# First block of an x-times-weight product reordered by kind of product, with a zero product ahead of it, in a shared-plus-routed expert kernel

## The chip, the cores and the metric

The kernel runs on one core of one Trainium2 chip. The metric is the device time of one execution in microseconds (us); of several runs the median is given. One further execution was recorded by the hardware profiler, and all rows below are from that one.

The engines are named as in the profile: PE is TensorE (matmul), PEld its weight load, DVE is VectorE, ACT is ScalarE, POOL is GpSimd, SP is SyncE, which here only issues DMAs. A q behind a name (SPq) is the engine's instruction queue issuing a DMA.

## The reference

The input x is 4 x 1024 tokens of 512 numbers. Two layers are added to it:

```
ys  = cond / sqrt(512)                                # [4, 512]
d   = rsqrt((ys*ys) @ (W*W) + 1e-8)                   # demodulation, [4, 512]
x1  = x + ((x * ys) @ W) * d                          # W is 512 x 512
shared = (silu(x1 @ w1) * (x1 @ w3)) @ w2             # 512 -> 1024 -> 512
s      = sigmoid([x1, cond] @ router_W)               # 8 experts
top 2 of s + bias per token, gates = s normalised over the two
routed = sum over the two experts of gate * (gelu(x1 @ W1e) @ W2e)
out = x1 + (shared + routed) / 3
```

All of it is fp32.

## The kernel before

Every large fp32 product is made of three products of fp32r operands: each operand is split into a high part (ACT copies it with rounding) and a low part (DVE subtracts the high part from the original), and PE adds high\*high, high\*low and low\*high in one bank of PSUM. So every tile of x, of a weight or of a hidden state passes ACT and then DVE before PE may use it.

**Stage 1, the first linear layer**: 8 blocks (NBLK) of 512 tokens. For a block, PE makes 4 output chunks o of 128 features, each from 4 input chunks c, three products each: 48 matmuls of 128x512. The first block is written apart in `first_linear` (loop over c outside, since its inputs arrive chunk by chunk), the others in `linear` (loop over o outside). Both call `part`, lines 416 to 418. After chunk c = 2 of the first block PE runs `demodulation` (line 399): 16 small fp32 products of the squared weight w0sq, made by POOL (line 1138), with the squared scales modsq. They show as 32 rows in the trace, with 4 columns each. ACT makes the weight's high parts wmh (line 583) and the block's high parts xh (`x_high`, line 575), and DVE the low parts wml (line 735) and xl (`scaled_low`, line 730). Before anything else both need mod, the scaled condition, which DVE makes (line 718) out of the load of cnd that SP issues first (line 235). ACT's queue waits for `prep` before its first high part.

The results leave PSUM by DVE at line 762 (x1t, one instruction for each o) into SBUF, PE then makes the router logits of the block (line 448), and SP stores x1t to HBM and loads the block after next into xin. In the last two blocks of the stage SP loads instead blocks 0 and 1 of the stored x1t back into xin, for stage 2; so in the last block (n = 7) ACT and DVE make the high and low parts of stage 2's first block (`x_low`, line 725). The tuple at line 764 says after which o DVE makes which low parts: none after o = 0 and 1, c = 0 after o = 2, and c = 1, 2, 3 after o = 3.

**Stage 2, the shared layer**: for each of 8 blocks, 8 hidden chunks hc. PE runs `up` (lines 468 to 470, 24 matmuls), then `down` of the hidden chunk before (lines 482 to 484, 12 matmuls). Between the two a hidden chunk passes ACT (silu, line 611), DVE (gate, line 792), ACT (high part gh, line 616) and DVE (low part gl, line 796). The order on each engine is fixed by the program; nothing is reordered at run time.

Beside it, ACT and DVE split the experts' weights for stage 3 in 32 pieces. In blocks 0 and 1 one piece goes with each hidden chunk: `piece_high` on ACT (line 631), `piece_low` on DVE (line 994), each at the end of the step of its hidden chunk. SP's `move_piece` loads a piece (line 302) and stores the split one (line 304). SP loads piece 0 at line 269, once the first two quarters of w2 are split. The load of a later piece needs that the piece two before it has been stored, since both use one buffer. In hidden chunk 1 of block 0 ACT also makes the router's sigmoid, for which it must load another table, and then the first one again for the silu after it. In block 1 DVE also works out the routing tables (lines 856 to 987).

**Stage 3, the routed experts**: 71 tiles of 128 gathered tokens, lines 530 to 532 on PE, with POOL gathering and scatter-adding rows.

Of the kernel before, what the change touches and what calls it, by code (L numbers as in the profile page):

```python
# [13 lines left out]
P = 128  # L14
# [51 lines left out]
def shared_moe_kernel(nc, xT, w0, condT, router_w, router_b, shared_w, expert_w, consts, tokid, padslots, padrows, out):  # L66
# [8 lines left out]
    with ctx:  # L75
        base = -(-nc.sbuf_base // 128) * 128

        def sb(name, shape, dt, kib):
            return nc.alloc_sbuf_tensor_at(name, [P] + shape, dt, offset=base + int(kib * KIB))
# [3 lines left out]


        x1t = sb("x1t", [2, DC, BLK], FP32, 0)
        w13 = sb("w13", [HC, 2, 2 * DC * P], FP32R, 16)
        wmh = sb("wmh", [2, DC, D], FP32R, 80)
        wml = sb("wml", [2, DC, D], FP32R, 96)
# [91 lines left out]
        cond_in = sem("cond_in")  # L180
        w0_in = [sem(f"w0_in{c}") for c in range(DC)]
        x0_in = [sem(f"x0_in{c}") for c in range(DC)]
        square_done = sem("square_done")
        pads_in = sem("pads_in")
        xin_in = [sem(f"xin_in{j}") for j in range(2)]
        wraw_in = [sem(f"wraw_in{j}") for j in range(2)]
# [44 lines left out]
        def _(sp):  # L231
            for j in range(2):
                sp.sem_inc(x1t_out[j], 16)
                sp.sem_inc(ehl_out[j], 16)
            sp.dma_start(cnd[:, :, :], condT).then_inc(cond_in, 16)
            for c in range(DC):
                sp.dma_start(w0s[:, c, :], w0[:, c, :]).then_inc(w0_in[c], 16)
            sp.sem_inc(xin_in[0], 16)
# [150 lines left out]
        def _(pe):  # L389
# [30 lines left out]
            def first_linear():  # L420

                for c in range(DC):
                    pe.wait_ge(wml_ready, c + 1)
                    pe.wait_ge(xl_ready, c + 1)
                    for o in range(DC):
                        last = part(0, o, c, 0)
                        if c == DC - 1:
                            last.then_inc(lin_done, 1)
                    if c == DC - 2:
                        demodulation()  # L430
# [12 lines left out]
            def logits(n, j):  # L443
# [5 lines left out]
                                         x1t[:, j, o, s * P:(s + 1) * P], start=(o == 0), stop=(o == DC - 1))  # L449
                last.then_inc(log_done, 1)  # L450

            first_linear()
            for n in range(1, NBLK):
                linear(n, n % 2)
# [117 lines left out]
        def _(act):  # L572
# [69 lines left out]
            for hc in range(HC):  # L642
                gate(0, hc)
                if hc == 1:
                    act.wait_ge(logit_done, 1)
                    act.activation(score[:, :, :], score[:, :, :], ACT.Sigmoid).then_inc(score_done, 1)
                next_high(0, hc, 0, NBLK // 2)
                hidden_high(0, hc)
                if hc in (0, 2, 4):
                    w2_high(1 + hc // 2)  # L650
                piece_high(0, hc)
            block_steps(1, 1, NBLK // 2 + 1)

            with act.Fori(1, NBLK // 2 - 1) as h:
# [48 lines left out]
        def _(dve):  # L703
# [10 lines left out]
            dve.sem_inc(xgt_done, 2)  # L714
            dve.sem_inc(hidt_done, 2)
            dve.sem_inc(ys_done, 2)
            dve.wait_ge(cond_in, 16)
            dve.tensor_scalar(mod[:, :, :], cnd[:, :, :], float(np.float32(1.0) / np.sqrt(np.float32(D))), None, ALU.mult).then_inc(prep, 1)
            dve.wait_ge(prep, 1)
# [13 lines left out]
            for c in range(DC):  # L733
                dve.wait_ge(wmh_ready, c + 1)
                dve.tensor_tensor(wml[:, 0, c, :], w0s[:, c, :], wmh[:, 0, c, :].bitcast(FP32), ALU.subtract).then_inc(wml_ready, 1)
                scaled_low(0, c)
            for c in range(DC):
                scaled_low(1, c)
            dve.wait_ge(small_in, 64)
# [13 lines left out]
            for n in range(NBLK):  # L753
                j = n % 2
                for o in range(DC):

                    dve.wait_ge(lin_done, DC * n + o + 1 + 1)
                    if o == 0:
                        dve.wait_ge(x1t_out[j], 16 * (n // 2) + 16)
                        if n > 1:  # L760
                            dve.wait_ge(log_done, n - 1)
                    dve.scalar_tensor_tensor(x1t[:, j, o, :], lin_ps[(DC * n + o) % 5][:, :], dsc[:, o, n // 2:n // 2 + 1],
                                             xin[:, j, o, :], ALU.mult, ALU.add).then_inc(x1t_done, 1)
                    for c in (() if n == 0 else ((), (), (0,), (1, 2, 3))[o]):
                        if n + 1 < NBLK:
                            scaled_low(n + 1, c)
                        else:
                            x_low(n + 1, (n + 1) % 2, c)
                dve.wait_ge(w_high, n + 1)
                dve.tensor_tensor(w13[:, n, 1, :], wraw[:, j, :], w13[:, n, 0, :].bitcast(FP32), ALU.subtract).then_inc(w_split, 1)  # L770
# [225 lines left out]
            for hc in range(HC):  # L996
                block_step(0, hc, 0, True)
                if hc < 2:
                    turn_x1(0, 0, 2 * hc)
                    turn_x1(0, 0, 2 * hc + 1)  # L1000
                if hc in (0, 2, 4):
                    w2_low(1 + hc // 2)
                if hc == 5:
                    dve.wait_ge(score_done, 1)
                    then(dve.tensor_tensor(row(SEL), score[:, :, :], per_expert(rb[:, :]), ALU.add))
                if hc == 6:
                    choose(0)
                if hc == 7:
                    choose(1)
                piece_low(0, hc)  # L1010
            for hc in range(HC):
                block_step(1, hc, 1, True)
                if hc == 0:
# [96 lines left out]
        def _(pool):  # L1110
# [22 lines left out]

                pool.wait_ge(xrow_out[i % XB], 16 * K * (i // XB + 1))

            for c in range(DC):
                pool.wait_ge(w0_in[c], 16)
                pool.tensor_tensor(w0sq[:, c, :], w0s[:, c, :], w0s[:, c, :], ALU.mult).then_inc(square_done, 1)
            pool.wait_ge(tables_done, 3)
            pool.wait_ge(sadr_done, K)  # L1140
            pool.wait_ge(pad_done, 1)
# [110 lines left out]
```

## Time and profile before

| | us |
|---|---|
| median of 3 runs | 1060.47 (1059.27 to 1061.65) |
| the profiled execution, its own time | 1054.4 |
| span of its trace (first to last instruction) | 1052.6 |
| PE busy in the span | 1021.2 |
| stage 1 on PE | 10.4 to 113.9 |
| stage 2 on PE | 115.8 to about 645 |
| stage 3 and the end | to 1052.6 |

The trace rows give a start and a duration in us from the start of the span. A matmul row's duration overlaps the next one's, so the pace of matmuls is read from the distance of their starts: 0.43 us at TensorE's clock of 1.2 GHz and 0.227 us at 2.4 GHz for 128x512. The profiled execution was 6.1 us shorter than the median of the runs; differences are made against its own rows and then taken off the median.

### The profile page before, as it was taken

What the parts mean: (1) busy time and instruction counts of PE and PEld (TensorE: products, weight loads), DVE (VectorE), ACT (ScalarE), POOL (GpSimd) and SP (SyncE); (2) the same over time, 40 slices, a digit from 0 to 9 for tenths busy, and PEclk for the clock granted to TensorE, in tenths of its full rate; (3) what the DMA queues carried; (4) which work ended last, traced back from release to release, by engine and by line L of the source; (5) the groups of instructions that cost most, each with busy time, mean ns of one, the idle gap of its engine ahead of it and who ended that gap; (6) DMA issues with size and microseconds to landing.
All of it is one profiled execution on the core that took longest, in us unless ns stands there. A gap on an engine that the chain in (4) does not pass through costs nothing.

```text
span 1052.6 us, 14602 instructions
## 1 busy us (share of the span) xinstructions
PE 1021.2 (97%) x4692; PEld 836.1 (79%) x4692; DVE 506.2 (48%) x828; ACT 293.0 (28%) x461; POOL 331.5 (31%) x393
## 2 busy tenths in 40 slices
PE   6999999999999999999999998999999999999996
PEld 5888778887888888888888886788888888878874
DVE  4555456668333333333322214555655566555653
ACT  3222252332222222122211112333333233332331
POOL 2000000001214433334312401365554645545533
PEclk9999999999999999999999999999999999999999
DMA  4666688787876677876833576999778999999984
GB/s 172 200 206 217 222 281 255 259 318 248 294 239 233 221 267 253 264 268 212 290 100 90 190 202 205 239 221 231 147 147 179 226 221 231 210 215 226 228 180 80
DMA packets 133259, 228.61 MB, mean 217 GB/s; under 512 B 29041, under 2 KB 83953, under 8 KB 125105
## 3 DMA queue, kind: packets, MB, share of 16 engines
q1 hardware_dynamic: 60400, 144.06, 42.8%
q0 software_dynamic: 31328, 64.11, 26.4%
q10 hardware_dynamic: 41472, 19.68, 7.9%
q8 instruction: 35, 0.57, 0.2%
q14 instruction: 24, 0.19, 0.1%
HBM read 112.85 MB, written 98.38 MB: 201 GB/s over the span
## 4 chain that ended last, share of the span: by engine, by line
PE 83%; DMA 8%; DVE 4%; SPq 2%; issue 2%; ACT 1%; POOLq 0%; DVEq 0%
PE banks L530 13%; PE banks L532 12%; PE banks L531 12%; PE banks L468 8%; PE banks L469 8%; PE banks L470 8%; DMA we_d<-ehl 5%; PE banks L482 4%; PE banks L483 4%; PE banks L484 4%; PE banks L416 3%; PE banks L417 3%; PE banks L418 3%; DMA eraw<-expert_w 2%; SPq L286 1%
## 5 line engine op out<-in xcount | busy, mean ns | idle before, releaser
L468 PE MATMUL banks<-xh,w 128*128 128x512 f32 x512 | 199.6, 390 | 1.8 <-DVE xl L725 1.8
L469 PE MATMUL banks<-xl,w 128*128 128x512 f32 x512 | 199.2, 389 | 0.0
L470 PE MATMUL banks<-xh,w 128*128 128x512 f32 x512 | 199.2, 389 | 0.0
L1184 POOL DMA_INDIRECT out<-ys,slot x71 | 124.0, 1746 | 181.1 <-DVE ys L1080 89.4
L792 DVE SCALAR_TENSOR_TENSOR gm<-sil,banks 128x512 f32<-128x512 f32 x64 | 43.9, 685 | 240.7 <-ACT sil L611 234.6
L1073 DVE TENSOR_TENSOR hidtl<-hidt,hidth 128x512 fp32r<-128x512 f32 x71 | 49.1, 692 | 165.9 <-ACT hidth L685 165.2
L611 ACT ACTIVATE sil<-banks 128x512 f32<-128x512 f32 x64 | 38.2, 597 | 291.9 <-PE banks L470 291.9
L1170 POOL DMA_DIRECT2D xg<-xs_d x136 | 99.9, 1108 | 58.8 <-DVE xgt L1054 49.6
L530 PE MATMUL banks<-we,hidth 128*128 x284 | 112.2, 395 | 5.8 <-issue 5.5
L530 PE MATMUL banks<-we,xgth 128*128 x284 | 111.1, 391 | 3.4 <-issue 3.4
L468 PEld LDWEIGHTS banks<-xh,w 128*128 128x128 f32 x512 | 96.1, 188 | 22.3 <-issue 2.3
L470 PEld LDWEIGHTS banks<-xh,w 128*128 128x128 f32 x512 | 96.1, 188 | 19.9
L469 PEld LDWEIGHTS banks<-xl,w 128*128 128x128 f32 x512 | 96.1, 188 | 19.8
L532 PE MATMUL banks<-we,hidtl 128*128 x284 | 110.7, 390 | 0.0
L531 PE MATMUL banks<-we,hidth 128*128 x284 | 110.7, 390 | 0.0
L531 PE MATMUL banks<-we,xgth 128*128 x284 | 110.5, 389 | 0.0
L532 PE MATMUL banks<-we,xgtl 128*128 x284 | 110.5, 389 | 0.0
L482 PE MATMUL banks<-wmh,gh 128*128 128x512 f32 x256 | 99.9, 390 | 2.8 <-DVE gl L796 1.7
L685 ACT ACTIVATE hidth<-hidt 128x512 fp32r<-128x512 f32 x71 | 44.9, 632 | 200.8 <-PE banks L532 131.1
L483 PE MATMUL banks<-wml,gh 128*128 128x512 f32 x256 | 99.6, 389 | 0.0
L484 PE MATMUL banks<-wmh,gl 128*128 128x512 f32 x256 | 99.6, 389 | 0.0
L1142 POOL DMA_DIRECT2D xrow<-padrows x1 | 0.8, 766 | 244.7 <-DVE place_of L987 244.7
(163 smaller groups left out, 1512.0 us busy)
## 6 DMA issues: line engine op xcount, KB each, us to landing
we_d<-ehl SPq DMA_DIRECT2D x32, 1024.0 KB, 7.3
we<-we_d SPq DMA_DIRECT2D x48, 512.0 KB
hturn<-hid ACTq DMA_DIRECT2D x284, 64.0 KB
xg<-xs_d POOLq DMA_DIRECT2D x136, 128.0 KB
eraw<-expert_w SPq DMA_DIRECT2D x32, 512.0 KB
x1t_d<-x1t SPq DMA_DIRECT2D x8, 1024.0 KB, 8.8
xin<-x1t_d SPq DMA_DIRECT2D x8, 1024.0 KB, 8.8
x_d<-x1tok SPq DMA_DIRECT2D x32, 256.0 KB
```

Of the source, the lines that this page charges most:

```text
L468: pe.matmul(ps[hc % 2][:, :], w_hi, xh[:, j, c, :], start=(c == 0), stop=False)
L469: pe.matmul(ps[hc % 2][:, :], w_hi, xl[:, j, c, :], start=False, stop=False)
L470: last = pe.matmul(ps[hc % 2][:, :], w_lo, xh[:, j, c, :], start=False, stop=(c == DC - 1))
L482: pe.matmul(o_ps[s][:, :], g_hi, w2h[:, hc, :], start=(hc == 0), stop=False)
L483: pe.matmul(o_ps[s][:, :], g_hi, w2l[:, hc, :], start=False, stop=False)
L484: last = pe.matmul(o_ps[s][:, :], g_lo, w2h[:, hc, :], start=False, stop=(hc == HC - 1))
L530: pe.matmul(ps, high[:, c, :], w_hi, start=(c == 0), stop=False)
L531: pe.matmul(ps, high[:, c, :], w_lo, start=False, stop=False)
L532: last = pe.matmul(ps, low[:, c, :], w_hi, start=False, stop=(c == DC - 1))
L1073: dve.tensor_tensor(hidtl[:, t % 2], hidt[:, t % 2], hidth[:, t % 2].bitcast(FP32), ALU.subtract).then_inc(hidt_done, 1)
L1170: pool.dma_start(xg[g * Q:(g + 1) * Q, m % 2 * PAIR:(m % 2 + 1) * PAIR].rearrange("p t a n -> p (t a) n"), xs_d[m * PAIR * P:(m + 1) * PAI ...
L1184: pool.indirect_dma_start(out[:, :], IO(slot[:, t, 0:1], 0), ys[:, t % RING, :], None, compute_op=ALU.add).then_inc(added[t % 2], 16)
```

## The change

1. **First block by kind of product.** `first_linear` issues for each c first the four products wmh\*xh (they wait for wmh and xh only), then the four wml\*xh (after a wait for wml), then the four wmh\*xl (after a wait for xl).
2. **Zeros.** DVE's first instruction fills a new tile of 128x512 with zeros (it shares its place with x1t), and PE starts with 20 matmuls of 128x512 on it, into the bank of lin_ps[4].
3. **Squares.** The four squares w0sq move from POOL to DVE, behind the low parts of the first block and ahead of those of the second.
4. **Condition.** The load of cnd is issued by POOL, no longer by SP ahead of the weight's loads.
5. **Low parts in the last block.** In block 7 of stage 1 DVE makes the low part c = o right after x1t of o, for each o.
6. **First piece.** Piece 0 of the experts' weights is split at the end of hidden chunk 1, right ahead of piece 1, and no longer at the end of hidden chunk 0, on ACT and on DVE.

```diff
+        zeros = sb("zeros", [BLK], FP32R, 0)
@@ sync
-            sp.dma_start(cnd[:, :, :], condT).then_inc(cond_in, 16)
@@ tensor
                 for c in range(DC):
+                    pe.wait_ge(wmh_ready, c + 1)
+                    pe.wait_ge(xh_ready, c + 1)
+                    for o in range(DC):
+                        pe.matmul(lin_ps[o][:, :], wmh[:, 0, c, o * P:(o + 1) * P], xh[:, 0, c, :], start=(c == 0), stop=False)
                     pe.wait_ge(wml_ready, c + 1)
+                    for o in range(DC):
+                        pe.matmul(lin_ps[o][:, :], wml[:, 0, c, o * P:(o + 1) * P], xh[:, 0, c, :], start=False, stop=False)
                     pe.wait_ge(xl_ready, c + 1)
                     for o in range(DC):
-                        last = part(0, o, c, 0)
+                        last = pe.matmul(lin_ps[o][:, :], wmh[:, 0, c, o * P:(o + 1) * P], xl[:, 0, c, :], start=False, stop=(c == DC - 1))
...
+            pe.wait_ge(zeros_done, 1)
+            for _ in range(20):
+                pe.matmul(lin_ps[4][:, :], zeros[:, 0:P], zeros[:, :], start=True, stop=True)
             first_linear()
@@ scalar
-                piece_high(0, hc)
+                if hc == 1:
+                    piece_high(0, 0)
+                if hc:
+                    piece_high(0, hc)
@@ vector
+            dve.memset(zeros[:, :].bitcast(FP32), 0.0).then_inc(zeros_done, 1)
             dve.wait_ge(cond_in, 16)
...
+            for c in range(DC):
+                dve.tensor_tensor(w0sq[:, c, :], w0s[:, c, :], w0s[:, c, :], ALU.mult).then_inc(square_done, 1)
...
-                    for c in (() if n == 0 else ((), (), (0,), (1, 2, 3))[o]):
+                    for c in (() if n == 0 else (o,) if n == NBLK - 1 else ((), (), (0,), (1, 2, 3))[o]):
...
-                piece_low(0, hc)
+                if hc == 1:
+                    piece_low(0, 0)
+                if hc:
+                    piece_low(0, hc)
@@ gpsimd
-            for c in range(DC):
-                pool.wait_ge(w0_in[c], 16)
-                pool.tensor_tensor(w0sq[:, c, :], w0s[:, c, :], w0s[:, c, :], ALU.mult).then_inc(square_done, 1)
+            pool.dma_start(cnd[:, :, :], condT).then_inc(cond_in, 16)
```

The order of instructions on PE at its start, before (the first 7 rows; "banks" are PSUM banks):

```order
L388 UNCONDITIONAL_BRANCH
L416 MATMUL banks<-xh,wmh 128x512
L417 MATMUL banks<-xl,wmh 128x512
L418 MATMUL banks<-xh,wml 128x512
L416 MATMUL banks<-xh,wmh 128x512
L417 MATMUL banks<-xl,wmh 128x512
L418 MATMUL banks<-xh,wml 128x512
```

and now:

```order
L388 UNCONDITIONAL_BRANCH
L460 MATMUL banks<-zeros 128x512 x20
L426 MATMUL banks<-xh,wmh 128x512 x4
L429 MATMUL banks<-xh,wml 128x512 x4
L432 MATMUL banks<-xl,wmh 128x512 x4
L426 MATMUL banks<-xh,wmh 128x512 x4
L429 MATMUL banks<-xh,wml 128x512 x4
L432 MATMUL banks<-xl,wmh 128x512 x4
```

The first product with xl stood second and now stands ninth among the products of the block, behind 20 of zeros.

The order on ACT from the first hidden chunk's high part on, before (ehl is the split piece, wmh here the high part of a quarter of w2):

```order
L631 ACTIVATE ehl<-eraw 128x1024
L611 ACTIVATE sil<-banks 128x512
L646 ACT_TABLE_LOAD
L646 ACTIVATE score<-score 128x256
L616 ACTIVATE gh<-gm 128x512
L631 ACTIVATE ehl<-eraw 128x1024
L611 ACT_TABLE_LOAD
```

and now:

```order
L620 ACTIVATE sil<-banks 128x512
L655 ACT_TABLE_LOAD
L655 ACTIVATE score<-score 128x256
L625 ACTIVATE gh<-gm 128x512
L640 ACTIVATE ehl<-eraw 128x1024 x2
L620 ACT_TABLE_LOAD
```

The piece that stood ahead of the silu of hidden chunk 1 now stands behind its high part gh.

## Rows read from the trace of the kernel before

**Rows 1.** PE's waits, whole span: us in total, times, longest.
```profile
PE banks L416 <- DVE xl L730: 10.4, 1, 10.4
...
PE banks L468 <- DVE xl L725: 1.8, 1, 1.8
PE banks L482 <- DVE gl L796: 1.7, 1, 1.7
PE banks L482 <- DVE outst L804: 1.0, 1, 1.0
```
**Rows 2.** Timeline from the start: start, duration, engine, line, what.
```profile
1.02 0.39 SPq L235 DMA_DIRECT2D cnd<-condT  x1
...
4.17 0.18 DVE L718 TENSOR_SCALAR mod<-cnd 128x16 f32<-128x16 f32 x1 [4.17 <-DMA cnd<-condT]
...
7.20 0.63 ACT L583 ACTIVATE wmh<-w0s 128x512 fp32r<-128x512 f32 x1 [2.40 <-DMA w0s<-w]
7.25 5.38 POOL L1138 TENSOR_TENSOR w0sq<-w0s 128x512 f32<-128x512 f32 x4 [6.79 <-DMA w0s<-w]
7.74 0.71 ACT L575 ACTIVATE xh<-xin,mod 128x512 fp32r<-128x512 f32 x1
...
8.76 1.52 DVE L730 SCALAR_TENSOR_TENSOR xl<-xin,mod,xh 128x512 fp32r<-128x512 f32 x1
...
10.43 0.77 PE L416 MATMUL banks<-xh,wmh 128*128 128x512 f32 x1 [10.43 <-DVE xl L730]
...
11.28 0.71 ACT L575 ACTIVATE xh<-xin,mod 128x512 fp32r<-128x512 f32 x1
...
14.37 0.68 DVE L735 TENSOR_TENSOR wml<-w0s,wmh 128x512 fp32r<-128x512 f32 x1
```
**Rows 3.** The same timeline: PE after its start.
```profile
14.27 0.39 PE L416 MATMUL banks<-xh,wmh 128*128 128x512 f32 x1
...
20.41 3.63 PE L399 MATMUL banks<-modsq,w0sq 128*128 128x4 f32 x32
```
**Rows 4.** Stretch: length, busy PE, PEld, DVE, ACT, POOL, then clock, DMA share, GB/s.
```profile
24.00:27.70 3.70, 3.70 (x11) 2.87 (x11) 2.63 (x8) 1.16 (x2) 0.00 (x0) 0.54 0.02 4
```
**Rows 5.** Chain of waits, end of block 0, start of block 2: start, duration.
```profile
28.27 0.23 PE banks L418
...
41.22 0.43 PE banks L416
```
**Rows 6.** ACT's timeline, third block's high parts.
```profile
36.20 2.56 ACT L575 ACTIVATE xh<-xin,mod 128x512 fp32r<-128x512 f32 x4 [10.75 <-DMA xin<-xT]
```
**Rows 7.** Timeline of the end of stage 1, ACT and DVE.
```profile
108.23 2.19 ACT L575 ACTIVATE xh<-xin 128x512 fp32r<-128x512 f32 x4 [8.36 <-DMA xin<-x1t_d]
...
112.94 0.75 DVE L762 SCALAR_TENSOR_TENSOR x1t<-banks,dsc,xin 128x512 f32<-128x512 f32 x1 [1.37 <-PE banks L418]
...
113.61 1.88 DVE L725 TENSOR_TENSOR xl<-xin,xh 128x512 fp32r<-128x512 f32 x3
...
115.75 0.47 PE L468 MATMUL banks<-xh,w 128*128 128x512 f32 x1 [1.84 <-DVE xl L725]
```
**Rows 8.** ACT's timeline in hidden chunks 0 and 1 of block 0.
```profile
133.36 1.06 ACT L631 ACTIVATE ehl<-eraw 128x1024 fp32r<-128x1024 f32 x1 [6.62 <-DMA eraw<-expert_w]
```
**Rows 9.** PE's timeline, the same place.
```profile
138.03 0.47 PE L482 MATMUL banks<-wmh,gh 128*128 128x512 f32 x1 [1.74 <-DVE gl L796]
```
**Rows 10.** SP's DMA issues, pieces 2 (load) and 1 (store).
```profile
139.59 0.33 SPq L302 DMA_DIRECT2D eraw<-expert_w  x1
140.23 0.35 SPq L304 DMA_DIRECT2D we_d<-ehl  x1
```
**Rows 11.** Chain of waits, 112 to 270 us: shares by line.
```profile
by line: DMA we_d<-ehl 34.5%; DMA eraw<-expert_w 10.1%; SPq L286 7.0%; DVE ehl L994 4.5%; issue 3.3%; SPq L302 2.9%; ACT gh L616 2.4%; PE banks L468 2.3%; DVE gl L796 2.2%; PE banks L469 2.2%; ACT ehl L631 2.0%; PE banks L470 2.0%; DVE gm L
```
**Rows 12.** Stretch of the input loads, columns as in Rows 4.
```profile
12.00:14.00 2.00, 2.00 (x7) 1.52 (x6) 2.00 (x3) 0.27 (x1) 0.63 (x1) 1.00 0.99 401
```
**Rows 13.** DMA issues by kind: KB each, median us from issue to landing.
```profile
xrow<-padslots POOLq DMA_DIRECT2D x1, 1.0 KB, 6.9
```

More of the change, by code:

```diff
@@ L182, in shared_moe_kernel @@
         x0_in = [sem(f"x0_in{c}") for c in range(DC)]
-        square_done = sem("square_done")
+        square_done, zeros_done = sem("square_done"), sem("zeros_done")
         pads_in = sem("pads_in")
```

## The prediction

> **What bounds the kernel now.** I read PE's waits over the whole span first [rows 1]. PE waits for another engine four times in 1052.6 us: 10.4 us for its first input, 1.8 at the end of stage 1, 1.7 in the first hidden chunks of stage 2 and 1.0 at 262 us. So PE bounds nearly everything; whatever makes it reach the later stages sooner shortens the run, unless something that doesn't move with PE then holds it back. The change touches the first three waits, and the fourth matters for what part of the gain stays.
>
> Next I read the timeline from the start [rows 2]. The first product needs no low part, but the program waits for one: xh of chunk 0 is ready at 7.74 + 0.71 = 8.45 us, xl at 8.76 + 1.52 = 10.28, and PE starts at 10.43. Then the pace [rows 3]: PE's tenth matmul starts at 14.27, so nine took 3.84 us, 0.427 each, which is TensorE at its lower clock of 1.2 GHz after an idle stretch. The other 27 up to the small products at 20.41 took 6.14 us, 0.227 each, which is 2.4 GHz. After 3.63 us of small products the clock is down again: the granted clock of 24.0 to 27.7 is 0.54 [rows 4], and the last chunk's twelve matmuls need from 20.41 + 3.63 = 24.04 to 28.27 + 0.23 = 28.50 [rows 3, 5], 4.46 us where 12 x 0.227 = 2.73 would do.
>
> **Part by part.**
>
> *By kind of product, with the condition's load moved.* PE may start 0.15 us after xh (the distance from xl to the first product now): 8.45 + 0.15 = 8.60, 1.83 us earlier. At full clock a chunk takes 12 x 0.227 = 2.73 us. Inputs come faster: the last xh ends at 11.28 + 0.71 = 11.99 [rows 2], while PE wants it at 8.60 + 3 x 2.73 plus the small products, after 20 us. The low parts of chunk 0 are wanted 0.9 and 1.8 us after the start, at 9.5 and 10.4; even with xl as slow as now, 10.28, it is in time. SP's queue is 0.4 us freer without cnd (issued at 1.02 now, [rows 2]), but the DMA engines are full while the inputs land (share 0.99, [rows 12]), so I take nothing for it; bounds 0 and 0.4. Chunk 0's weight load lands shortly ahead of 7.20, and cnd at 4.17, so cnd has slack: mod, its square (0.18 each) and one small ACT instruction of about 0.2 have to be done by 7.20, so it may land up to 6.5.
>
> *Zeros.* DVE's memset can run about when SP issues its first DMA, 1.02 us. The trace has no memset of this size; its nearest row, a DVE operation of 128x512 with two inputs, is 0.68 [rows 2], and a tiny one 0.18. So the zeros on PE start at about 1.5. If TensorE's clock rises as it did, 3.84 us after the start, nine take 3.84 us and eleven 2.50: they end at 7.8, ahead of 8.60. If it never rose they would take 20 x 0.427 = 8.54 and end at 10.0. I take the first: then the nine slow matmuls of the block are gone, 3.84 - 9 x 0.227 = 1.80 us. The gap up to 8.60 is 0.8 us; PE idled for 1.84 and 1.74 us further on, and the first matmul behind them took 0.47 [rows 7, 9], not the 0.77 of the cold start [rows 2]; so such a gap keeps the clock.
>
> *Squares on DVE.* Four times 0.68 behind the last xl. That one ends about 0.1 + 0.74 after the last xh, at 12.9 (DVE is no longer slowed to 1.52 beside POOL; 0.74 for one is my estimate from 0.68), so the squares are done at 15.6, and PE comes to them at 8.60 + 36 x 0.227 = 16.8. Cost nothing; without that 1.2 us of cover each microsecond would be one of PE's. The low parts of block 1 come 2.7 us later, at about 18.6; PE wants them after the last chunk, at about 24.9.
>
> *The clock after the small products.* They stay where they are, 3.63 us of 4-column matmuls, so I leave the dip in: gain 0, with 4.46 - 2.73 = 1.73 as the other bound. First block in all: 1.83 + 1.80 = **3.6 us**. The results now come out together at the end of the last chunk, so x1t of o = 3 is some 2 us later against PE than now, and with it the reload of xin, on which ACT's high parts of block 2 wait (they start at 36.20 and take 2.56, [rows 6]). Their shift is 1.5 us instead of 3.6. PE starts block 2 at 41.22 [rows 5] and needs the second low part three matmuls on, at 41.9 - 3.6 = 38.3. The second high part ends at 36.20 - 1.5 + 1.28 = 36.0, and behind it DVE has x1t of o = 3 and then this low part, 0.75 and 0.74 at most: 37.5. Cost nothing, with little to spare: 0.8 us.
>
> *Last block of stage 1.* Now three low parts stand behind the last x1t: 113.61 + 1.88 = 115.49, PE 115.75 [rows 7]. With one (a third, 0.63 to 0.68) they end at 114.3 and PE starts at 114.55: **1.2 us**. The cost is a wait: DVE, after x1t of o = 0, stands until ACT's first high part at about 108.23 + 0.6 = 108.8, with x1t of o = 1 to 3 queued behind. Six operations of 0.6 to 0.7 (low, x1t, low, x1t, low, and room) follow by 112.2, and x1t of o = 3 isn't due before 112.94. Cover 0.7 us; beyond it, the reload being late costs one for one.
>
> *First piece.* ACT's piece 0 waits for its load until 133.36 [rows 8], ahead of the silu of hidden chunk 1, and for the low part gl of that chunk PE waits 1.74 us, until 138.03 [rows 9]. Moved behind, silu to gl need no DMA and the wait goes: 1.7 us. But what follows in blocks 0 and 1 is not PE's pace: in the chain from 112 to 270 us the DMAs of pieces hold 34.5 + 10.1% [rows 11], and it ends in DVE's routing tables and outst at 262, for which PE already waits 1.0 us. This chain starts at piece 0's load, which shifts with stage 1's gains but not with this one. Its first links: piece 1 is stored at 140.23, and could be at best shortly after 139.59, when piece 0's buffer is free [rows 10]. So the chain gains some 0.3, PE comes 1.7 earlier, and the wait of 1.0 grows to about 2.4. I take **0.3 us**, bounds 0 and 1.7.
>
> **Sum**: 1.83 + 1.80 + 1.2 + 0.3 = 5.1 us. The profiled execution's 1054.4 becomes 1049.3. The median of the runs was 1060.47; I take the same difference off it: **1055.4**.
>
> **A page against the trace.** The dip after the small products is what the row shows [rows 4]. The Trainium skill (TensorE: Matmul & The Clock Gate, Part 1) says the gate's observation runs freely and isn't tied to the kernel's start. By that rule, with the small products now 3.6 us earlier, the dip can fall otherwise or not at all; no row here shows it.
>
> **The rivals.**
>
> *A. The clock stays up through the small products.* They begin 16.8 us in, with work on both sides. Then 1.73 us more: 6.8 in all, 1053.7. Against it: the same products in the same length did bring it down. Chance 0.17.
>
> *B. Zeros don't raise the clock.* They end at 10.0, the block starts there, 0.4 us earlier than now, and its nine slow matmuls remain: 0.4 + 1.2 + 0.3 = 1.9 us, 1058.6. For it: no row shows a product of zeros. Against: PE's array has the same work to do. Chance 0.09.
>
> *C. The gain is taken back later.* A chain beside PE (pieces in blocks 0 and 1, weights in stage 3) doesn't shift with stage 1. Then PE's wait at 262 grows by the whole gain, to about 6 us, and the time is 1060 to 1060.5. Against: piece 0's load waits for w2's parts, which follow PE. Chance 0.08.
>
> *D. Slower: the condition on POOL's queue.* Everything on ACT stands behind mod. If cnd lands later than 6.5, each microsecond is one of start. The nearest row of that queue is 6.9 from issue to landing [rows 13]: landing at about 8, a loss of 1.5, still a gain of 3.6 in all. It turns if its packets must wait until the input loads are through (still 0.99 busy at 12 to 14, [rows 12]). Landing at 15: the start comes 8.5 us later than forecast, and the clock has fallen in the idle stretch, 1.8 more. 5.1 - 10.3 = -5.2: 1065.7. It decides from a landing at 11.6 on. Chance 0.04. The Trainium skill (DMA: Bandwidth & Descriptors, Latency and other measured facts) puts the first byte of a POOL-issued DMA at 1 us against 0.6, so by the page it would be only 0.4 later, within the slack.
>
> **How the numbers follow.** Forecast 0.62, A 0.17, B 0.09, C 0.08, D 0.04. About 2.1 us (0.2%) is what a measurement of this kernel can tell from no change. Forecast and A are faster, of B half (it stands at the bound), C is the same: faster 0.84, same 0.12, slower 0.04. The range: at the lower end A with the piece's 1.7 kept, 1060.5 - 8.2 = 1052.3, less 1.3 for the spread of the runs; at the upper end B with 1.2 of spread. Range 1051.0 to 1059.8; D and part of C lie outside.
>
> **What would show it.** In the profile after: zeros from about 1.5 to 7.8 with the step from 0.43 to 0.227 between; the first real product at 8.6 and 0.227 apart; small products at about 16.8, again a clock near 0.54 behind them; end of the first block at 24.9; PE's wait ahead of up at 0.6 or less; no wait at line 482 for gl near 134, and one of about 2.4 us for outst near 258. Wrong would be: cnd landing after 6.5, zeros at 0.43 throughout, a PE wait for x1t or xl in block 2, or a wait for outst of 1.0 (then the piece's gain is whole).

## The result and the profile after

| | before | changed |
|---|---|---|
| median of 8 runs, us | 1061.18 (1058.67 to 1065.06) | 1055.68 (1052.02 to 1060.37) |
| ratio | | 0.9945, 95% interval 0.992 to 0.997 |
| profiled execution, span | 1052.6 | 1058.6 |

The changed kernel is faster by 5.5 us, by the interval 3.2 to 8.5. The forecast of 1055.4 lies 0.3 us off the median; that it is so near is partly luck, as the terms show below. But the one profiled execution of the changed kernel is 6 us longer than that of before, so the sum can't be read off two spans; it has to be followed from stage to stage.

PE's waits over the whole span (us in total, times, longest), which answer to [rows 1]:

```profile
PE banks L539 <- issue: 12.0, 22, 2.3
PE banks L491 <- DVE outst L819: 3.0, 2, 2.1
PE banks L460 <- DVE zeros L729: 1.9, 1, 1.9
PE banks L539 <- SPq L340: 1.5, 1, 1.5
PE banks L477 <- DVE xl L738: 0.6, 1, 0.6
PE banks L426 <- ACT xh L584: 0.6, 1, 0.6
```

The wait for gl is gone, the one for xl is 0.6 instead of 1.8, and the one for outst has grown from one of 1.0 to two of 3.0 together. The start, from the timeline (start, duration, engine, line, what), against [rows 2]:

```profile
1.32 0.75 POOL L1154 DMA_DIRECT2D cnd<-condT  x1 [0.85 <-POOLq L1262]
1.40 0.48 DVE L729 MEMSET zeros<- 128x512 f32 x1 [1.40 <-PEq L1262]
1.94 6.98 PE L460 MATMUL banks<-zeros 128*128 128x512 f32 x20 [1.94 <-DVE zeros L729]
...
7.57 0.17 DVE L731 TENSOR_SCALAR mod<-cnd 128x16 f32<-128x16 f32 x1 [5.69 <-DMA cnd<-condT]
...
8.63 0.70 ACT L584 ACTIVATE xh<-xin,mod 128x512 fp32r<-128x512 f32 x1
...
9.48 1.16 PE L426 MATMUL banks<-xh,wmh 128*128 128x512 f32 x4 [0.56 <-ACT xh L584]
...
17.75 4.56 PE L399 MATMUL banks<-modsq,w0sq 128*128 128x4 f32 x32
```

The condition lands 6.2 us after POOL issues it, at 7.5 instead of 4.1, and ACT's first high part, which no longer waits for the weight, waits for it: the block starts at 9.48, not at 8.60. Then it runs at full pace at once (four products in 1.16). After the small products comes the dip, in stretches as in [rows 4] (length, busy PE, PEld, DVE, ACT, POOL, then granted clock, DMA share, GB/s):

```profile
17.80:20.00 2.20, 2.20 (x22) 2.20 (x21) 1.38 (x3) 0.00 (x0) 0.00 (x0) 1.00 0.00 0
20.00:22.20 2.20, 2.20 (x14) 2.20 (x13) 0.00 (x0) 0.00 (x0) 0.00 (x0) 0.55 0.03 7
...
25.70:27.20 1.50, 1.50 (x5) 1.18 (x4) 0.74 (x2) 0.00 (x0) 0.00 (x0) 0.55 0.00 0
```

It begins already among the small products, which take 4.56 us instead of 3.63, and takes in all twelve products of the last chunk: the clock is at half from 20.2 to 27.1 us, against 24.3 to 27.7 in the kernel before.

**Milestones on PE**, us from the span's start (first row of each kind), for the two kernels and for the two repetitions described below:

| | before | before again (f1) | changed | changed again (e1) |
|---|---|---|---|---|
| first real product | 10.43 | 10.54 | 9.48 | 9.25 |
| logits of the condition (after block 1) | 39.24 | 39.29 | 38.17 | 36.37 |
| first product of stage 2 | 115.75 | 115.80 | 113.48 | 111.68 |
| first product of stage 3 | 643.89 | 643.99 | 641.91 | 640.09 |
| from there to the end of the span | 408.7 | 411.5 | 416.7 | 412.1 |

Stages 1 and 2 repeat to 0.1 us in the kernel before, and differ by 1.8 us in the changed one. Stage 3 scatters by 8 us; in the longest of these four the chain of waits runs through its DMAs and scatter-adds:

```profile
1019.96 4.30 DMA out<-ys,slot
...
1030.68 5.42 DMA out<-ys,slot
```

So all runs below are read by these milestones first, and by their times second.

### The profile page after: what moved, and what is told of

The parts are those of the page before. It is cut to its first block, busy times and chain, and to the rows that moved or that the text cites. A ratio compares the mean times of both kernels' runs of the same rounds, so it can differ in the third digit from the quotient of the medians.

```text
span 1058.6 us, 14641 instructions
## 1 busy us (share of the span) xinstructions
PE 1031.7 (97%) x4712; PEld 842.4 (80%) x4712; DVE 505.7 (48%) x833; ACT 292.0 (28%) x461; POOL 332.0 (31%) x390
## 4 chain that ended last, share of the span: by engine, by line
PE 69%; DMA 17%; issue 4%; DVE 4%; SPq 2%; POOL 1%; ACT 1%; ACTq 1%; POOLq 0%; DVEq 0%
PE banks L539 11%; PE banks L540 10%; PE banks L541 10%; PE banks L477 6%; PE banks L479 6%; PE banks L478 6%; DMA we_d<-ehl 6%; DMA we<-we_d 4%; PE banks L491 3%; PE banks L493 3%; PE banks L492 3%; PE banks L416 3%; PE banks L417 2%; PE banks L418 2%; DMA xs_d<-xrow,sadr 2%
```

## The experiments

Twelve experiments ran, two of them repetitions, each with 5 rounds of timed runs (9 or 12 runs of each). Ratios are against the kernel before on the same chip. "After" in the diffs is the changed kernel.

**e1, the changed kernel again.**

> The changed kernel once more, to see what repeats. Theory M (stages 1 and 2 carry the gain, stage 3 only scatters): first real product within 0.3 us of 9.5, up to the first product of stage 2 at 113.5 +- 2 depending on where the clock falls, first product of stage 3 at 642 +- 2, and the length of stage 3 anywhere in 407 to 417 us; time 1053 to 1058. Rival S (the change also shortens stage 3): stage 3 here is 404 to 406 us.

1053.75 us against 1058.31, ratio 0.9951 (0.9933 to 0.997). Milestones as above: theory M holds, stage 3 isn't shortened (412.1). The dip here starts only behind the small products and ends inside the next block:

```profile
19.00:21.00 2.00, 2.00 (x20) 2.00 (x20) 0.97 (x3) 0.00 (x0) 0.00 (x0) 1.00 0.03 8
21.00:23.00 2.00, 2.00 (x9) 1.67 (x9) 1.13 (x6) 1.17 (x2) 0.00 (x0) 0.81 0.00 0
23.00:25.00 2.00, 2.00 (x6) 1.54 (x6) 0.70 (x2) 0.00 (x0) 0.00 (x0) 0.50 0.00 0
25.00:26.00 1.00, 1.00 (x5) 0.78 (x4) 1.00 (x3) 0.00 (x0) 0.00 (x0) 0.67 0.00 0
```

Same program, same work, 1.8 us between the two. Of that, 0.2 us is the start; the other 1.6 is the dip, which lasted from 22.3 to 25.7 us here and from 20.2 to 27.1 in the first trace. So it is mainly how long the clock stayed down, and not only where it fell.

**e2, the condition's load on SP.**

```diff
+            sp.dma_start(cnd[:, :, :], condT).then_inc(cond_in, 16)
             for c in range(DC):
                 sp.dma_start(w0s[:, c, :], w0[:, c, :]).then_inc(w0_in[c], 16)
...
-            pool.dma_start(cnd[:, :, :], condT).then_inc(cond_in, 16)
```

> The changed kernel with the condition's load issued by SP again, ahead of the weight's loads. Theory Q (POOL's queue delivers the condition late, at 7.5 us, and that costs the start): the first real product at 8.6 +- 0.2, 0.9 us earlier than in the changed kernel, and the first product of stage 2 earlier by about as much if the clock falls at the same place. Rival W (the start is set by the weight's first load, which SP now issues 0.4 us later): first real product still at 9.2 to 9.5.

Its timeline from the start:

```profile
1.95 6.47 PE L461 MATMUL banks<-zeros 128*128 128x512 f32 x20 [1.95 <-DVE zeros L730]
...
4.06 0.18 DVE L732 TENSOR_SCALAR mod<-cnd 128x16 f32<-128x16 f32 x1 [2.17 <-DMA cnd<-condT]
...
6.97 0.63 ACT L593 ACTIVATE wmh<-w0s 128x512 fp32r<-128x512 f32 x1 [2.27 <-DMA w0s<-w]
...
7.50 0.71 ACT L585 ACTIVATE xh<-xin,mod 128x512 fp32r<-128x512 f32 x1
```

Theory Q holds: the condition is there at 4.1, ACT waits for the weight again, xh ends at 8.21, and PE starts at 8.36, 1.1 and 0.9 us ahead of the two traces of the changed kernel. Moving this one small load cost the start about 1 us. But e2 puts back two things at once: the queue, and the place ahead of the weight's loads. Other small loads in the changed kernel's trace, issued by SP behind the weight's, were as slow (DMA issues by kind: KB each, median us from issue to landing):

```profile
rw<-router_w SPq DMA_DIRECT2D x1, 32.0 KB, 7.5
cnd<-condT POOLq DMA_DIRECT2D x1, 8.0 KB, 6.2
rb<-router_b SPq DMA_DIRECT2D x1, 4.0 KB, 6.3
```

In the kernel before, SP's rb took 5.9 us too, while cnd, which SP issued first of all, took 3.1. So the place behind the large loads may explain all of it. The load on SP behind the weight's, which would tell the two apart, wasn't run. The time, 1055.02 (ratio 0.9957, 0.9938 to 0.9976), doesn't show it: this trace had the long dip (logits of the condition at 37.02), and a microsecond is less than the interval.

**e3, no zeros.**

```diff
-            pe.wait_ge(zeros_done, 1)
-            for _ in range(20):
-                pe.matmul(lin_ps[4][:, :], zeros[:, 0:P], zeros[:, :], start=True, stop=True)
```

> The changed kernel without its 20 products of zeros. Theory Z (the zeros raise the clock): the block's first 8 to 10 products 0.427 us apart, the small products start 1.8 us later than in the changed kernel, at 19.6, and stage 2 starts up to 1.8 us later, less if the dip behind the small products becomes shorter. Rival (the first products would be at the higher clock anyway): small products at 17.8.

PE's timeline at its start:

```profile
9.32 2.04 PE L426 MATMUL banks<-xh,wmh 128*128 128x512 f32 x4 [9.32 <-ACT xh L581]
11.16 1.72 PE L429 MATMUL banks<-xh,wml 128*128 128x512 f32 x4
```

Theory Z holds: the first four products take 1.84 us from start to start instead of about 1.0, and the small products come at 19.08, against 17.54 in e1 and 17.75. From the first real product to the first small one it is 9.76 us, against 8.29 and 8.27: 1.5 us. So products of zeros raise the clock as products of data do. What is left at stage 3 is less clear: it starts at 640.76, between the two traces of the changed kernel, since the dip behind was a short one and the waits for outst were 2.1 us instead of 3.0. Time 1054.63, ratio 0.9974 (0.9954 to 0.9993); the intervals of e1 and e3 overlap.

**e4, the small products dealt out.**

```diff
                     for o in range(DC):
                         pe.matmul(lin_ps[o][:, :], wmh[:, 0, c, o * P:(o + 1) * P], xh[:, 0, c, :], start=(c == 0), stop=False)
+                        if c == DC - 1:
+                            next(small, None)
...
+                        if c == DC - 1:
+                            next(small, None)
+                            next(small, None)
...
-                    if c == DC - 2:
-                        demodulation()
+                        if c == DC - 2:
+                            next(small, None)
```

(`small` is the list of the 16 products, taken one by one; the first four stand behind the last four matmuls of chunk 2.)

> The changed kernel with the 16 small products of the demodulation dealt out among the last four matmuls of chunk 2 and the first eight of chunk 3, one or two behind each. Theory D (a stretch of nothing but 4-column products lets the clock fall): no granted clock under 0.9 between 15 and 30 us, and the first block ends at 24.6 or sooner, against 27.3 in the changed kernel. Rival (the small products are as light wherever they stand, so the mixed stretch lets the clock fall too): clock near 0.5 again for some 3 us, end of the first block 26.5 or later.

The stretches behind chunk 2, columns as above:

```profile
17.00:19.00 2.00, 2.00 (x16) 1.80 (x14) 2.00 (x4) 0.91 (x2) 0.00 (x0) 1.00 0.01 4
19.00:21.00 2.00, 2.00 (x17) 1.84 (x15) 0.30 (x2) 0.00 (x0) 0.00 (x0) 1.00 0.04 8
21.00:23.00 2.00, 2.00 (x17) 1.86 (x17) 0.00 (x0) 0.00 (x0) 0.00 (x0) 1.00 0.00 0
23.00:25.00 2.00, 2.00 (x11) 1.70 (x11) 1.23 (x7) 1.17 (x2) 0.00 (x0) 1.00 0.00 0
```

No dip; the first block ends at 24.15 (theory D asked for 24.6 or sooner), logits of the condition at 35.04, stage 3 at 637.17. Time 1053.6, ratio 0.9951 (0.9933 to 0.997), the same as e1's on the same chip: the timed runs don't show this gain. By itself one trace proves little, as f4 below shows; g1 to g4 repeat it.

**f1, the kernel before again.**

> The kernel before once more, unchanged. Theory L (the one trace of before that the forecast used was a fast one in stages 1 and 2, since the clock's dip varied): the first product of stage 3 comes later than that trace's 643.9 us, by up to 1.5 us. Rival: 643.9 +- 0.3, and what the timed runs show beyond 2 to 4 us lies in stage 3.

Theory L falls: 643.99, as in the first trace. Time 1060.32 against 1058.82 on that chip, ratio 1.0016 (0.9996 to 1.0036): this much two sets of runs of one kernel differ.

**f2, the first piece in its old place.**

```diff
-                if hc == 1:
-                    piece_high(0, 0)
-                if hc:
-                    piece_high(0, hc)
+                piece_high(0, hc)
```

and the same for `piece_low`.

> The changed kernel with the first piece split at the end of hidden chunk 0 again. Theory G (what the moved piece gains is given back at the wait for outst near 258): the wait for gl of 1.7 us near 134 is back, the waits for outst near 190 and 258 shrink together from 2.9 to about 1.2, and from the first product of stage 2 to the first of stage 3 it takes 528.4 +- 0.4 us as in the changed kernel. Rival K (the gain is kept): the waits for outst stay near 2.9 and that stretch takes 530.1.

PE's timeline where it waits in stage 2:

```profile
134.13 0.47 PE L491 MATMUL banks<-wmh,gh 128*128 128x512 f32 x1 [1.86 <-DVE gl L808]
...
258.40 0.50 PE L491 MATMUL banks<-wmh,gh 128*128 128x512 f32 x1 [0.73 <-DVE outst L816]
```

Theory G holds: the wait for gl is back (1.86), the one near 190 is gone and the one near 258 is 0.73 (1.2 was expected). From the first product of stage 2 to the first of stage 3 it takes 528.00 us, against 528.43 and 528.41 in the changed kernel, and 528.14 and 528.19 in the kernel before. What the moved piece gains at 134 is given back in full. The 0.4 us between f2 and the changed kernel says nothing more: with the piece moved and stage 2 otherwise the same program, this stretch was 526.8 to 528.5 us over seven traces (changed, e1 to e4, g3, g4), 528.0 in the mean; with the piece in its old place it was 528.0 to 528.2 in three. Time 1057.27, ratio 0.9982 (0.9954 to 1.0009), which is the slowest of the variants. Its trace doesn't say why (stage 3 was 407.9). Its timed runs also had the lowest granted clock of all variants, 0.993 in the median against 0.995 in e1, but whether that explains it is open.

**f3, the old low parts in the last block.**

```diff
-                    for c in (() if n == 0 else (o,) if n == NBLK - 1 else ((), (), (0,), (1, 2, 3))[o]):
+                    for c in (() if n == 0 else ((), (), (0,), (1, 2, 3))[o]):
```

> The changed kernel with the low parts of the last block of stage 1 in their old places. Forecast's theory: PE waits 1.8 us for xl ahead of stage 2, against 0.6, so from the first logits of the condition to the first product of stage 2 it takes 76.5 us, against 75.3. The 1.2 us are kept to stage 3, because the chain of pieces starts behind it. Rival: the early low parts only move a wait, and the stretch stays at 75.3 to 75.6.

The stretch from the logits of the condition to stage 2 takes 76.51 us, as in both traces of before, against 75.3 in the changed kernel and all its other variants: 1.20 us, as forecast. Part of it may not last: the waits for outst were 0.6 us less here, in one trace. And stage 2 held a surprise. It took 529.67 us, and not for waits (2.4 us for outst, against 3.0 in the changed kernel). PE's timeline at the start of stage 2, and the stretches from there, columns as above:

```profile
114.89 0.47 PE L477 MATMUL banks<-xh,w 128*128 128x512 f32 x1 [1.84 <-DVE xl L738]
```

```profile
115.00:116.00 1.00, 1.00 (x5) 0.82 (x6) 1.00 (x2) 0.00 (x0) 0.00 (x0) 1.00 0.96 311
116.00:117.00 1.00, 1.00 (x5) 0.76 (x4) 1.00 (x2) 0.00 (x0) 0.00 (x0) 0.60 1.15 295
117.00:118.00 1.00, 1.00 (x4) 0.81 (x3) 0.01 (x1) 0.00 (x0) 0.00 (x0) 0.50 0.83 188
```

About a microsecond behind the idle stretch of 1.84 us (ahead of which PE ran a microsecond of router logits) the clock fell to half, until about 119.6. That cost about 1.8 us: 529.67 - 528.43 + 0.56. The two traces of before have the same gap without this dip [rows 7], and none of the eleven traces with a gap of 0.6 us there has it. One case in three is a hint that the longer gap is to blame; it doesn't show it. Time 1056.43, ratio 0.9976 (0.9958 to 0.9994).

**f4, the tables earlier.**

```diff
-                if hc == 5:
+                if hc == 3:
                     pe.wait_ge(mask_done, 1)
-                    pe.wait_ge(gm_done, HC + 4 + 1 + 2)
+                    pe.wait_ge(gm_done, HC + 2 + 1 + 2)
...
-                if hc == 5:
-                    first_slots()
-                if hc == 6:
-                    slot_rows()
-                    pad_rows()
-                if hc == 7:
-                    turns()
-                    tile_tables()
+                if hc == 3:
+                    first_slots()
...
+                if hc == 7:
+                    tile_tables()
```

(slot_rows, pad_rows and turns at hc 4, 5 and 6; the rank is taken over at hc 2.)

> The changed kernel with the routing tables of block 1 made two hidden chunks earlier and spread over five (rank at chunk 3, then one part of the tables at each chunk). Theory V (the wait for outst near 258 is set by VectorE's table work behind a late piece): that wait falls from 2.0 to under 0.3 us and stage 3 starts 1.5 to 2 us earlier. Rival P (the pieces' DMAs alone set it): it stays at 1.5 or more.

The wait near 258 stays at 1.64 us: rival P. Behind it stands the piece on both engines, in ScalarE's and VectorE's timelines:

```profile
250.43 1.06 ACT L640 ACTIVATE ehl<-eraw 128x1024 fp32r<-128x1024 f32 x1 [8.35 <-DMA eraw<-expert_w]
```

```profile
251.53 1.22 DVE L1009 TENSOR_TENSOR ehl<-eraw,ehl 128x1024 fp32r<-128x1024 f32 x1 [5.83 <-ACT ehl L640]
...
254.66 2.48 DVE L819 TENSOR_TENSOR outst<-banks,xres 128x512 f32<-128x512 f32 x4
```

VectorE was free 5.83 us ahead of it, waiting for ScalarE, and that 8.35 us for the load. And this trace has no dip after the small products, which stand together as in the changed kernel (they took 3.63 us, logits of the condition at 34.92). Time 1054.06, ratio 0.9958 (0.9933 to 0.9982).

**g1 to g4** all have the small products dealt out as in e4.

**g1** adds f4's tables and moves the last pieces of blocks 0 and 1 behind the output:

```diff
                 if hc == 0:
                     output(0)
+                    piece_low(0, HC - 1)
...
+                            if 2 * h + j == 2:
+                                piece_low(1, HC - 1)
```

with ScalarE's `piece_high` in the matching place.

> The changed kernel with the small products dealt out as in e4, the tables made earlier as in f4, and the last pieces of blocks 0 and 1 split behind the outputs of the block before, in hidden chunk 0 of the next block, no longer ahead of them (the loops over blocks 2 to 5 on ScalarE and VectorE are written out for that). Theory H (a late piece, standing ahead of the output on both engines, sets both waits for outst): both waits are under 0.3 us, and from the first product of stage 2 to the first of stage 3 it takes 525.5 +- 0.6 us, against 528.4; stage 3 starts at 635.5 to 636.5. Rival R (the residual's load or the pieces' DMAs hold the output themselves): waits for outst of 1 us or more remain. For the clock: by theory D no dip between 15 and 30 us, a second case beside e4.

From PE's waits over the span:

```profile
PE banks L499 <- DVE gl L821: 0.7, 1, 0.7
```

No wait for outst is left, only this one for gl; stage 2 takes 525.80 us, 2.6 less than in the changed kernel and 1.0 less than the shortest of the seven traces named at f2. Theory H holds: a late piece ahead of the output made both waits. The tables alone don't remove them (f4 kept 1.23 us near 189 and 1.64 near 257); whether the moved pieces would without the tables wasn't run. 1052.41 us, ratio 0.9943 (0.9916 to 0.997).

**g2** is g1 with e2's edit.

> g1 with the condition's load on SP. By theories Q, D and H together: first real product at 8.4 to 8.6, no dip, first product of stage 3 at 634.5 to 635.5, 7 us ahead of the changed kernel's first trace, and a time 3 to 6 us under the changed kernel's. Rival (what is gained by stage 3 is lost in it, since its length follows its DMAs): stage 3 takes 412 us or more and the time is that of the changed kernel, 1053 to 1056.

No wait for gl or outst at all, stage 2 in 524.88 us, stage 3 from 634.84: 7.1 us ahead of the changed kernel's first trace and 9.1 ahead of before. 1050.76 us, ratio 0.9923 (0.9895 to 0.995): the lowest of all, 8 us under the kernel before. Stage 3 took 414.1 us in its trace, so the rival's first half came true, but the time stayed under its 1053 to 1056: g3, which ran on the same chip with the late pieces and the tables in their old places, took 1053.28. The start fell short, see g3.

**g3** is the changed kernel with e4's and e2's edits alone.

> The changed kernel with the small products dealt out and the condition's load on SP, nothing else. Theories Q and D: first real product at 8.4 to 8.6, no dip between 15 and 30 us, logits of the condition at 34.0 +- 0.3, against 38.2 and 36.4 in the two traces of the changed kernel. Rival to D (it was chance that e4 had no dip, as f4 had none with the small products together): a granted clock near 0.5 somewhere between 15 and 30 us here or in g1, g2 or g4.

Its timeline from the start:

```profile
1.94 7.33 PE L469 MATMUL banks<-zeros 128*128 128x512 f32 x20 [1.94 <-DVE zeros L738]
...
8.06 0.71 ACT L593 ACTIVATE xh<-xin,mod 128x512 fp32r<-128x512 f32 x1
...
9.11 1.08 PE L430 MATMUL banks<-xh,wmh 128*128 128x512 f32 x4
```

No dip, logits of the condition at 34.53, 0.5 us later than expected. PE started at 9.11 though xh was ready at 8.77, since the 20 zeros ran until then (a row's duration overlaps the next one's); in g2 they held the start to 9.24 with xh ready at 8.11. How long 20 zeros take depends on when the clock rises: 6.33 us in e1, 7.46 in g2. With the condition on SP they can be too many: in e2, where they took 6.47, they cost nothing. 1053.28 us, ratio 0.9945 (0.9923 to 0.9967).

**g4** is the changed kernel with e4's edit and the squares on POOL, behind the condition's load:

```diff
             pool.dma_start(cnd[:, :, :], condT).then_inc(cond_in, 16)
+            for c in range(DC):
+                pool.wait_ge(w0_in[c], 16)
+                pool.tensor_tensor(w0sq[:, c, :], w0s[:, c, :], w0s[:, c, :], ALU.mult).then_inc(square_done, 1)
```

> The changed kernel with the small products dealt out and the four squares on GpSimd again, behind the condition's load. Theory C (VectorE's operations with two inputs run at half pace beside GpSimd's): wml and xl of the first chunks take 1.0 to 1.5 us instead of 0.69 and 0.75, as in the kernel before, but PE doesn't wait, since xl comes third: the first block ends within 0.3 us of e4's, at 24.0 +- 0.3. Rival: PE waits for a low part in the first two chunks and the block ends 1 us or more later.

VectorE's timeline from the start, with the square that GpSimd (POOL) made at the same time:

```profile
7.19 1.05 POOL L1163 TENSOR_TENSOR w0sq<-w0s 128x512 f32<-128x512 f32 x1 [0.31 <-DMA w0s<-w]
7.31 0.95 DVE L739 TENSOR_SCALAR mod<-cnd 128x16 f32<-128x16 f32 x1 [5.42 <-DMA cnd<-condT]
...
10.56 0.69 DVE L756 TENSOR_TENSOR wml<-w0s,wmh 128x512 fp32r<-128x512 f32 x1
11.16 1.53 DVE L751 SCALAR_TENSOR_TENSOR xl<-xin,mod,xh 128x512 fp32r<-128x512 f32 x1
12.61 1.52 DVE L756 TENSOR_TENSOR wml<-w0s,wmh 128x512 fp32r<-128x512 f32 x1
```

Two of the low parts take 1.5 us, as in the kernel before, and PE doesn't wait for them: theory C. One thing it didn't have: the tiny mod instruction, 0.17 us elsewhere, took 0.95 beside POOL's square, and all of the start hung on it: PE started at 10.00, and the logits of the condition came at 35.53, 0.5 us after e4's. 1053.47 us, ratio 0.9956 (0.9932 to 0.9981).

**The dip, counted over all traces.** With the small products together, it came in 8 of 9 traces (before, f1, changed, e1, e2, e3, f2, f3; not in f4). With them dealt out, it came in none of 5 (e4, g1 to g4). Counted from the first real product to the logits of the condition, which takes the start out, what the dip costs can be read off directly:

| | traces | us |
|---|---|---|
| long dip, as in the changed kernel (20.2 to 27.1 us) | changed, e2, f3 | 28.7 |
| short dip, as in e1 (22.3 to 25.7 us) | e1, f2 | 27.1 |
| no dip, small products together | f4 | 25.5 |
| no dip, small products dealt out | e4, g1 to g4 | 25.4 to 25.5 |
| without zeros, short dip | before, f1, e3 | 28.6 to 28.8 |

A short dip costs 1.6 us and a long one 3.2. Dealing the small products out costs nothing of its own.

The timed runs list a granted clock too, the mean over the run. In the experiments and the changed kernel it was 0.997 or more in 42 of 54 runs with the small products dealt out, and in 16 of 92 with them together, which agrees with the count over the traces. Their times are another matter. With the small products dealt out and stage 2 unchanged the ratios are 0.9951 (e4), 0.9945 (g3) and 0.9956 (g4), against 0.9945 and 0.9951 in the two sets of the changed kernel. What is gained by dealing out, 1.6 to 3.2 us in the traces, is not clear of the noise of these medians.

## Why the prediction was right, point by point

The forecast of 5.1 us met the timed 5.5 (and 4.6 in e1). The mechanisms held in the main, but the near match is partly luck: the terms add to about 3.6 us in the traces, not 5.1. They came out as follows.

**Start, 1.83 forecast: 0.95 and 1.2 measured.** The step that failed is "cnd has slack ... it may land up to 6.5". It landed at 7.5 (e1: 7.3). This was rival D's mechanism at small size, and its nearest row, 6.9 us on POOL's queue [rows 13], was the better guide than the 3.1 us that SP's needed; the landing took 6.2. Whether POOL's queue or the place behind the weight's loads made it late is open (e2). e2 gives back 0.9 to 1.1. The sentence of the Trainium skill (DMA: Bandwidth & Descriptors, Latency and other measured facts) on the first byte, 1 us for POOL against 0.6, didn't cover it: with the load also moved behind others, and the DMA engines 0.90 to 0.99 busy until it landed, the difference was 3 us. The forecast for the zeros was short as well: they were to end at 7.8, and their rows end between 8.3 and 9.4. The late condition hid that; with it on time they held PE back in g2 and g3.

**Clock at the start, 1.80 forecast: 1.7 against the kernel before, 1.5 by e3.** From the first real product to the first small one it was 9.98 us before and 8.27 and 8.29 in the changed kernel. Rival B is out. The squares on DVE and block 2 cost nothing, as forecast: PE has no wait for either.

**The dip, left in at 0 with 1.73 as the other bound.** This is the term that varied. Five traces have the changed kernel's first block unaltered (changed, e1, f2, f3, f4): the logits of the condition came at 38.17, 36.37, 36.41, 38.38 and 34.92, against 39.24 and 39.29. The gain up to there was 0.9 to 4.3 us, 2.4 in the mean, where 3.6 was forecast; rival A happened in one of the five. In the two traces of the changed kernel the parts (start, clock at the start, dip) add up: 0.95 + 1.71 - 1.59 = 1.07 us in the first, whose long dip cost 1.6 us more than the short one of before, and 1.18 + 1.69 + 0.00 = 2.87 in e1. The forecast's bounds, 0 and 1.73, left out that the dip can also get longer; this was so in two of the five (changed, f3). That the observation isn't tied to the kernel's start, as the Trainium skill says (TensorE: Matmul & The Clock Gate, Part 1), agrees with this spread of dips for one and the same program.

**Last block of stage 1, 1.2 forecast: 1.20**, by f3 and by both traces of before. A slip in the working had no effect: six operations of 0.6 to 0.7 us from 108.8 end at 112.4 to 113.0, not by 112.2, so the cover of 0.7 us could have been nothing.

**First piece, 0.3 forecast: about 0.** The single traces say -0.2 to -0.4, but the mean of the seven traces named at f2 is 0.1 us under that of the three with the piece in its old place. The mechanism was right: PE came earlier, the chain of pieces didn't, and the wait for outst took it back (3.0 instead of 1.0). The place was half right: I put it at 258 alone, and 0.9 us of it fell at 192, at the output of block 0. And I named "DVE's routing tables" as what ends that chain; f4 shows that without them the piece's load holds it as well, and g1 that with the piece moved behind the output as well it goes.

**Sum.** With the mean of the first block, 2.4 + 1.2 + 0 = 3.6 us at the start of stage 3; the two traces of the changed kernel show 2.0 and 3.8. The timed gains of 5.5 and 4.6 us have intervals that reach down to 3.2, so this is no contradiction, but it lies at their lower end. A cause of more was seen but not shown: a dip behind a gap of 1.84 us (f3). The kernel before has two such gaps [rows 7, 9], and the change shortens one to 0.6 us and removes the other. No trace of before had this dip, so it is open how often it costs there. In the timed runs the kernel before had a granted clock of 0.994 in the mean and the changed kernel, in its two sets, 0.995. That is the right direction, but small; whether stage 3 adds something is open too, since its length went from 407.9 to 417.0 us over the 14 traces with no order that I can name. In 7 of them the clock also fell to half for some us between 1031 and 1044, but those aren't the longer ones (412.8 us in the mean, against 411.7).

**"Such a gap keeps the clock"**, said of 0.8 us with the gaps of 1.84 and 1.74 as evidence, held for the gap ahead of the first block (0.6 and 1.0 us), but the evidence was weaker than it looked: f3 had a dip behind 1.84.

## What to carry to other kernels

Read a gain at milestones along the bounding engine, in more than one trace, before comparing spans: here one stage repeats to 0.1 us and another scatters by 8. A wait that is removed in a stretch paced by DMAs only moves to the next output; what helped was to take the late transfer's work out of the way of the output. Dealing small products out among large ones removed the clock's dip in every trace and cost nothing; here that was worth 1.6 to 3.2 us in the traces, too little for the timed runs to show. A tiny load that everything depends on was quick when it was issued first, ahead of the input loads. A filler of fixed length, such as the 20 zeros, needs slack for a late rise of the clock.

## What the runs showed of the hardware that was not expected

- 32 rows of 4-column matmuls in a row (3.63 us) brought TensorE's clock to half in 8 of 9 traces; the same 32 among twelve 128x512 products in none of 5. It fell 2.5 to 4.7 us after the first of them, and in three of the eight it stayed down twice as long as in the other five; both differed between executions of one program.
- An 8 KB load issued by POOL behind the first input loads took 6.2 us to land, and 3.1 when SP issued it first. A 4 KB load issued by SP behind them took 5.9 to 7.0.
- Products of zeros raised the clock as products of data do; 20 of them took 6.33 to 7.46 us, by when it rose.
- A 128x16 VectorE instruction with one input took 0.95 us instead of 0.17 beside a GpSimd square (g4).
